# Row maxima one step later, turn and projections exchanged, seven PSUM banks for the last scores

## The chip, the cores and the metric

The kernel runs on one core of a Trainium2 chip. The metric is the device time of one execution in microseconds (us), the median of several. The core's engines work from queues of their own and wait for each other by semaphores: TensorE (PE; its weight loads are PEld), VectorE (DVE), ScalarE (ACT), GpSimd (POOL) and SyncE (SP), which issues most DMAs.

## The reference, cut to what matters

Sixteen sequences of 512 tokens, 128 features, 16 heads of 8 elements. Attention whose weights are the mean of the softmax and the softmax with key 0 taken out; output projection; residual; layer norm. Then a layer of eight experts, two for each token, and a second residual and layer norm.

```python
Q, K, V = heads(x @ Wq.T + bq), heads(x @ Wk.T + bk), heads(x @ Wv.T + bv)
probs = softmax(Q @ K.T / sqrt(8))
cut = probs with key 0 set to 0, divided by its sum
x1 = layernorm(x + ((probs + 0.5 * (cut - probs)) @ V) @ Wo.T + bo)
for e in 8 experts:   # wte: weights of the two chosen experts
    out += wte[:, e] * ((silu(x1 @ w1[e].T) * (x1 @ w3[e].T)) @ w2[e].T)
result = layernorm(x1 + out)
```

## The kernel before, in words

**Units and periods.** A unit is four heads of one sequence (`UNITS` is 64; unit u is group g = u % 4 of sequence b = u // 4). The loop runs over periods p from -2 to 63, each of eight steps k; two steps, an even and the odd one after it, are called a pair below. In period p the engines take the exponentials of unit p (16 score blocks of 128 keys by 512 queries, two to a step), the products with the values of unit p - 1 (four 128-key chunks, one in each odd step), and the row maxima of unit p + 2 (four parts of 128 queries, one in each even step).

**Row maxima.** A part is four matmuls of 32 contracted rows into the four banks of `mx_ps` (L635) and one VectorE reduction over all four banks (L1019). There is one such set of banks: the matmuls of a part wait for the reduction of the part before, and the reduction waits for the matmuls. When a unit's four parts are reduced, PE turns them to rows (`negmax_to_rows`, L666, "the turn"), ACT copies them (L846), POOL splits them in two bf16 parts (`split_negmax`, L1383 and L1385), and SP moves them by two 4 KB DMAs (`move_negmax`, L485) to two rows of the query operand. The first score matmul of the unit waits for that move (`s_m_loaded`).

**Order within a step.** It is written out: on PE the maxima of an even step, one score, the values of an odd step, the second score, the turn, and then one small piece named in `BEHIND` by (g, k), or in `ONCE` for the first periods: `q0` to `k1` are halves of a later sequence's projections, `v0`, `v1` value halves, `wo0`, `wo1` output halves, `px` prefix sums, `gc`, `gw` products for the gate. Scores, turns and pieces share a ring of three PSUM banks in order (`ring_at`, `bank_of`); ACT empties each bank, and PE waits for the emptying three entries back.

**Before the loop proper.** In periods -2 and -1 there are maxima and no scores; PE runs eight spare matmuls behind each part (L727). The piece `q0` of sequence 2 in period -1 needs the load of that sequence's `xT`, which SP issues behind the loads of the score operands of units 0 and 1 (L421 behind L478 and L479).

**GpSimd.** Its work of a period lies in four slots. A slot begins when PE has finished that step's maxima (`beside_reduction(p, w)`), so that it runs while VectorE reduces from PSUM. In periods of group 0, slot 1 holds the split of the maxima and a scatter, slot 2 holds `split_rest` (L1405, L1407) of a later sequence. VectorE runs routing operations of an earlier sequence after the reductions (L1077, L1081, L1086 in group 0).

**SyncE.** In order in each period: the move, loads of x or xT or the storing of split projections, the score operands of unit p + 5, the maxima operands of unit p + 4.

**After the loop.** In periods 62 and 63 there are no maxima. VectorE works out the table of expert tiles (`first_tables`, `tile_steps`, `tile_rows`), SP then loads the first rows, VectorE turns them (L1295), ACT copies the first weights, and PE goes on with the expert tiles, whose first product (`tile_up`, L755) writes into `mx_ps`.

Of the kernel before, what the change touches and what calls it, by code (L numbers as in the profile page):

```python
# [25 lines left out]
P = 128  # L26
# [32 lines left out]
def layer(nc, xT, x, wqT, wkT, wvT, woT, bq, bk, bv, bo, gateT, w1T, w3T, w2T, out):  # L59
# [16 lines left out]
    with ctx:  # L76
# [199 lines left out]
        UNITS, STEPS = NB * NG, 2 * QC  # L276
        PERIODS = range(-2, NB * NG)
# [4 lines left out]
        def is_seq(b):  # L282
            return 0 <= b < NB

        BEHIND = {(0, 3): ("k1", 2), (1, 3): ("v0", 1), (1, 5): ("v1", 1), (1, 7): ("px", -2),
                  (2, 5): ("wo0", -1), (2, 7): ("wo1", -1), (3, 3): ("q0", 3), (3, 5): ("q1", 3), (3, 7): ("k0", 3)}
# [11 lines left out]
        for p in PERIODS:  # L300
            for k in range(STEPS):
# [4 lines left out]
                if k == 1 and is_unit(p + 1):  # L306
                    ring_at["mT", p + 1] = ring_count
                    ring_count += 1
# [17 lines left out]

        def half(name):
            return slice(L // 2 * int(name[1]), L // 2 * (int(name[1]) + 1))

        def bank_of(n):  # L330
            return ring_ps[n % 3 if n < TAIL else 2][:, 0, :]
# [284 lines left out]
        def _(pe):  # L616

            def ring_bank(*what):

                n = ring_at[what]  # L620
                if n >= 3:
                    pe.wait_ge(s_ring_done, n - 2 if n < TAIL else n)
# [95 lines left out]
            for p in PERIODS:  # L718
                b, g = divmod(p, NG)
                for k in range(STEPS):  # L720
                    c = k // 2
                    if k % 2 == 0 and is_unit(p + 2):
                        maxima(p + 2, c)
                        if p + 2 in (0, 1):

                            for n in range(8):
                                nc.tensor.matmul(acc_ps[:, 0, :], QM[p + 2][:, 0:P], KM[p + 2][:, :], start=True, stop=True)  # L727
# [11 lines left out]
                    if k == 1 and is_unit(p + 1):  # L739
# [83 lines left out]
        def _(act):  # L823
# [100 lines left out]
            for p in PERIODS:  # L924
                b, g = divmod(p, NG)
                for k in range(STEPS):
# [3 lines left out]
                    if k == 1 and is_unit(p + 1):  # L930
# [54 lines left out]
        def _(dve):  # L985
# [226 lines left out]
            for p in PERIODS:  # L1212
                b, g = divmod(p, NG)
                for k in range(STEPS):
                    if k == 0 and is_unit(p - 2):
                        sums_by_query(p - 2)
                    if k % 2 == 0 and is_unit(p + 2):
                        maxima(p + 2, k // 2)
# [126 lines left out]
        def _(pool):  # L1345
# [235 lines left out]
            beside_reduction(-1, 1)  # L1581
# [4 lines left out]
            for p in PERIODS[2:]:  # L1586
# [3 lines left out]
                if g == 0:  # L1590
# [3 lines left out]
                    beside_reduction(p, 1)  # L1594
                    if is_unit(p + 1):
                        split_negmax(p + 1)
                    scatter_chunk(b - 3, 0)
                    beside_reduction(p, 2)
# [6 lines left out]
                elif g == 1:  # L1605
# [5 lines left out]
                    if is_unit(p + 1):  # L1611
                        split_negmax(p + 1)
# [3 lines left out]
                    beside_reduction(p, 2)  # L1616
                    if is_seq(b - 1):
# [7 lines left out]
                elif g == 2:  # L1625
# [5 lines left out]
                    if is_unit(p + 1):  # L1631
                        split_negmax(p + 1)
# [112 lines left out]
```

## Time and profile before

| | |
|---|---|
| median of 3 runs | 1175.48 us (1175.12 to 1177.51) |
| profiled execution | 1174.36 us, of which the span from the first to the last instruction is 1171.9 |
| PE busy | 1117.2 us (95%) |
| DVE busy | 911.3 us (78%) |
| ACT busy | 824.7 us (70%) |
| POOL busy | 689.8 us (59%) |

The shares are means over stages that differ. The second part of the page shows them over time, each digit the busy share of a fortieth of the span in tenths; PEclk is TensorE's granted clock:

```profile
PE   9999999999999999999999999999999999999996
DVE  6888999999999999999999999854545554444545
ACT  2588888888889889888889888853544344344537
PEclk9999999999999999999999999999999999999998
```

The main loop ends in slice 27 (about 764 us); until there PE and DVE are both nearly full, after it PE alone.

### The profile page before, as it was taken

The numbers are of one execution on the slowest core, as the hardware profiler recorded it, in microseconds if no ns is written. First come the engines' busy times: TensorE is split into PE (matmuls) and PEld (weight loads), VectorE is DVE, ScalarE is ACT, GpSimd is POOL, SyncE is SP. The second block draws the span as 40 slices with busy tenths as digits, with TensorE's granted clock in tenths as the row PEclk, the third lists the DMA queues.
The fourth block names the chain that finished last, engine by engine and source line by source line (L and its number), as shares of the span: only waits on it lengthen the run. The fifth ranks groups of instructions, "written<-read, shape, count | busy, mean of one in ns | idle before, by whom it ended". The sixth has DMA issues, their size and how long they took to land.

```text
span 1171.9 us, 23608 instructions
## 1 busy us (share of the span) xinstructions
PE 1117.2 (95%) x7240; PEld 575.9 (49%) x7240; DVE 911.3 (78%) x1309; ACT 824.7 (70%) x1668; POOL 689.8 (59%) x1131
## 2 busy tenths in 40 slices
PE   9999999999999999999999999999999999999996
PEld 6422232222222222222322222279999999999962
DVE  6888999999999999999999999854545554444545
ACT  2588888888889889888889888853544344344537
POOL 4424557777777776777777755676645434334336
PEclk9999999999999999999999999999999999999998
DMA  4453334444334343443444345353434433332257
GB/s 147 147 158 111 109 119 125 129 124 132 126 122 132 123 131 108 144 123 116 136 121 133 123 136 166 93 117 80 94 78 99 90 78 76 76 75 59 59 158 299
DMA packets 175051, 139.79 MB, mean 119 GB/s; under 512 B 89539, under 2 KB 151623, under 8 KB 174928
## 3 DMA queue, kind: packets, MB, share of 16 engines
q1 hardware_dynamic: 165672, 119.95, 36.4%
q0 software_dynamic: 8688, 18.14, 4.6%
q8 instruction: 60, 0.98, 0.4%
q14 instruction: 63, 0.52, 0.1%
q10 hardware_dynamic: 568, 0.20, 0.1%
HBM read 95.96 MB, written 42.19 MB: 118 GB/s over the span
## 4 chain that ended last, share of the span: by engine, by line
PE 54%; DVE 37%; issue 6%; DMA 1%; ACT 1%; ACTq 0%; POOL 0%; SPq 0%; POOLq 0%; DVEq 0%
DVE rowmax_sb L1019 32%; PE ring_ps L786 10%; PE mx_ps L755 10%; PE mx_ps L765 10%; PE ring_ps L646 6%; PE acc_ps L658 6%; PE mx_ps L635 4%; DVE TN_sb L1028 3%; PE mx_ps L817 2%; PE ring_ps L693 1%; PE ring_ps L676 1%; PE acc_ps L717 1%; PE ring_ps L817 1%; PE acc_ps L727 1%; DVE attnT_sb L1046 0%
## 5 line engine op out<-in xcount | busy, mean ns | idle before, releaser
L840 ACT ACTIVATE probs_sb<-ring_ps 128x512 f32<-128x512 f32 x1024 | 558.4, 598 | 96.0 <-PE ring_ps L646 80.7
L1019 DVE TENSOR_REDUCE rowmax_sb<-mx_ps 128x4 f32<-128x2048 f32 x256 | 586.5, 2291 | 40.9 <-PE mx_ps L635 32.6
L646 PE MATMUL ring_ps<-region_sb 74*128 74x512 bf16 x1024 | 311.4, 384 | 2.1 <-ACT probs_sb L840 2.0
L658 PE MATMUL acc_ps<-probs_sb,values_sb 128*32 128x512 f32 x2048 | 272.3, 604 | 0.0
L1694 POOL DMA_INDIRECT y_d<-probs_sb,values_sb x135 | 133.1, 986 | 183.8 <-DVE probs_sb L1313 159.3
L646 PEld LDWEIGHTS ring_ps<-region_sb 74*128 74x128 bf16 x1024 | 79.3, 97 | 312.8 <-ACT probs_sb L840 272.4
L915 ACT ACTIVATE xT_sb<-region_sb 128x512 f32 x78 | 49.2, 630 | 183.2 <-PE mx_ps L765 181.8
L1313 DVE SCALAR_TENSOR_TENSOR probs_sb<-ring_ps,values_sb 128x128 f32<-128x128 f32 x135 | 42.2, 347 | 147.3 <-issue 126.3
L1547 POOL DMA_INDIRECT rows_d<-sent_sb,pos_sb x128 | 130.3, 1018 | 40.2 <-issue 19.2
L635 PE MATMUL mx_ps<-k_maxima_sb,q_maxima_sb 32*128 32x512 bf16 x1024 | 101.0, 385 | 39.4 <-DVE rowmax_sb L1019 39.0
L786 PE MATMUL ring_ps<-region_sb,probs_sb 128*128 x1080 | 134.1, 276 | 0.3 <-DVE probs_sb L1323 0.3
L786 PEld LDWEIGHTS ring_ps<-region_sb,probs_sb 128*128 128x128 f32 x1080 | 131.0, 192 | 3.7 <-issue 0.5
L755 PE MATMUL mx_ps<-k_parts_sb,xT_sb 128*128 128x256 f32 (+1 forms) x624 | 130.2, 351 | 0.0
L1323 DVE TENSOR_TENSOR probs_sb<-mx_ps,probs_sb 128x512 f32<-128x512 f32 (+1 forms) x156 | 95.4, 619 | 25.4 <-PE mx_ps L765 17.7
L755 PEld LDWEIGHTS mx_ps<-k_parts_sb,xT_sb 128*128 128x128 f32 x624 | 106.8, 191 | 12.4 <-DVE k_parts_sb L1295 0.8
L658 PEld LDWEIGHTS acc_ps<-probs_sb,values_sb 128*32 128x32 f32 x2048 | 40.5, 108 | 97.7 <-issue 97.4
L635 PEld LDWEIGHTS mx_ps<-k_maxima_sb,q_maxima_sb 32*128 32x128 bf16 x1024 | 25.7, 91 | 110.7 <-DVE rowmax_sb L1019 101.8
L961 ACT ACTIVATE probs_sb<-mx_ps 128x1024 f32<-128x1024 f32 (+1 forms) x78 | 70.4, 903 | 3.5 <-PE mx_ps L755 3.4
L765 PE MATMUL mx_ps<-k_parts_sb,full_q_sb 128*128 128x256 f32 (+1 forms) x312 | 65.5, 353 | 0.0
L765 PE MATMUL mx_ps<-k_parts_sb,full_k_sb 128*128 128x256 f32 (+1 forms) x312 | 64.6, 350 | 0.0
L1383 POOL CAST negmax_parts_sb<-negmax_sb 16x128 bf16<-16x128 f32 x64 | 17.9, 280 | 64.4 <-PE mx_ps L635 64.2
L765 PEld LDWEIGHTS mx_ps<-k_parts_sb,full_q_sb 128*128 128x128 f32 x312 | 51.6, 191 | 5.3 <-issue 0.8
(197 smaller groups left out, 1182.2 us busy)
## 6 DMA issues: line engine op xcount, KB each, us to landing
region_sb<-q_parts_d SPq DMA_DIRECT2D x64, 288.0 KB
region_sb<-k_parts_d SPq DMA_DIRECT2D x64, 288.0 KB
k_parts_d<-k_parts_sb SPq DMA_DIRECT2D x46, 256.0 KB, 2.5
k_maxima_sb<-k_parts_d SPq DMA_DIRECT2D x128, 64.0 KB
probs_sb<-y_d SPq DMA_DIRECT2D x32, 256.0 KB, 6.8
q_maxima_sb<-q_parts_d SPq DMA_DIRECT2D x126, 64.0 KB
values_sb<-rows_d SPq DMA_DIRECT2D x57, 132.0 KB
q_parts_d<-q_parts_sb SPq DMA_DIRECT2D x15, 384.0 KB, 3.6
```

The source lines that it names most:

```text
L635: last = nc.tensor.matmul(mx_ps[:, j, :], q[rows, P * c:P * (c + 1)], k[rows, :], start=True, stop=True)
L646: nc.tensor.matmul(bank, KS[b % 2][0:KR + MR, h, P * c:P * (c + 1)], QS[b % 2][0:KR + MR, h, :], start=True, stop=True).then_inc(s_ring_re ...
L658: last = nc.tensor.matmul(acc_ps[VW * j:VW * (j + 1), 0, :], VE[b % 2][:, c, HG * g + j, :], PT[u % 2][:, j, c, :], start=(c == 0), stop=( ...
L755: last = nc.tensor.matmul(up_ps[:, c, 0:n], W1T[t % 2][:, P * c:P * (c + 1)], XGT[t % 2][:, 0:n], start=True, stop=True)
L765: last = nc.tensor.matmul(lin_ps[:, c, 0:n], W3T[t % 2][:, P * c:P * (c + 1)], XGT[t % 2][:, 0:n], start=True, stop=True)
L786: last = nc.tensor.matmul(y_ps[:, at:at + D], HH[t % 2][:, c, P * w:P * (w + 1)], W2[:, bass.ds(expert + c * D, D)], start=(c == 0), stop= ...
L840: nc.scalar.activation(PT[u % 2][:, i // QC, i % QC, :], ring_bank("st", u, i), ACT.Exp, scale=SCALE).then_inc(s_ring_done, 1)
L961: nc.scalar.activation(SG[t % 2][:, :, 0:n], up_ps[:, :, 0:n], ACT.Silu).then_inc(s_silu, 1)
L1019: V.tensor_reduce(rowmax[u % 2][:, :].rearrange("p (j c) -> p j c", c=QC)[:, :, c], mx_ps[:, :, :], axis=AXX, op=ALU.max, negate=True).the ...
L1323: V.tensor_tensor(HH[t % 2][:, part, 0:n], lin_ps[:, part, 0:n], SG[t % 2][:, part, 0:n], ALU.mult)\
L1547: G.indirect_dma_start(rows_d, bass.IndirectOffsetOnAxis(ap=pos[b % 2][:, s, c:c + 1], axis=0), XE[b % 2][:, c, s, :], None).then_inc(s_sc ...
L1694: G.indirect_dma_start(y_d, bass.IndirectOffsetOnAxis(ap=XG[t % RING][:, w, D:D + 1].bitcast(i32), axis=0), YO[t % YRING][:, w, :], None, ...
```

## The change: what it does, and the diff

Each maxima part comes one even step later: part c of period p is now part 7 + c of the unit count (`maxima_at`), so period p holds the last part of unit p + 1 and the first three of unit p + 2. The first one falls on step 2 of period -2, behind `gc`; the last one on step 0 of period 62. The turn goes from step 1 to step 3, and the pieces `k1`, `v0`, `q0` go from step 3 to step 1 of their periods. POOL's split of the maxima goes from slot 1 to slot 2. The scores of units 62 and 63 but the last six go over seven banks, the three of the ring and the four of `mx_ps`; the first four that use `mx_ps` wait for all reductions, and the first expert product waits for the last of these scores to be emptied.

```diff
+        LEAD = 2 * QC - 1
+        def maxima_at(p, c):
+            n = QC * p + c + LEAD
+            return divmod(n, QC) if 0 <= n < QC * UNITS else (None, None)
-        BEHIND = {(0, 3): ("k1", 2), (1, 3): ("v0", 1), (1, 5): ("v1", 1), (1, 7): ("px", -2),
-                  (2, 5): ("wo0", -1), (2, 7): ("wo1", -1), (3, 3): ("q0", 3), (3, 5): ("q1", 3), (3, 7): ("k0", 3)}
+        BEHIND = {(0, 1): ("k1", 2), (1, 1): ("v0", 1), (1, 5): ("v1", 1), (1, 7): ("px", -2),
+                  (2, 5): ("wo0", -1), (2, 7): ("wo1", -1), (3, 1): ("q0", 3), (3, 5): ("q1", 3), (3, 7): ("k0", 3)}
-                if k == 1 and is_unit(p + 1):        # ring_at, PE and ACT: the turn
+                if k == 3 and is_unit(p + 1):
+        WIDE = range(ring_at["st", UNITS - 2, 0], TAIL - 6)
+        banks_at = [WIDE[0] % 3, (WIDE[0] + 1) % 3, (WIDE[0] + 2) % 3, 3, 4, 5, 6]
+        def bank_no(n):
+            return banks_at[(n - WIDE[0]) % 7] if n in WIDE else n % 3
+        def last_in_bank(n):
+            return max(m for m in range(n) if bank_no(m) == bank_no(n))
         def bank_of(n):
-            return ring_ps[n % 3 if n < TAIL else 2][:, 0, :]
+            bank = bank_no(n) if n < TAIL else 2
+            return ring_ps[bank][:, 0, :] if bank < 3 else mx_ps[:, bank - 3, :]
             def ring_bank(*what):                    # PE
-                if n >= 3:
-                    pe.wait_ge(s_ring_done, n - 2 if n < TAIL else n)
+                if n in WIDE[3:7]:
+                    pe.wait_ge(s_mx_done, QC * UNITS)
+                elif n >= 3:
+                    pe.wait_ge(s_ring_done, last_in_bank(n) + 1 if n < TAIL else n)
-                    if k % 2 == 0 and is_unit(p + 2):  # PE; DVE alike
-                        maxima(p + 2, c)
-                        if p + 2 in (0, 1):
+                    u, part = maxima_at(p, c)
+                    if k % 2 == 0 and u is not None:
+                        maxima(u, part)
+                        if p < 0:
                             for n in range(8):
...
             def tile_up(t):
                 if t >= 1:
                     pe.wait_ge(s_silu, t)
+                else:
+                    pe.wait_ge(s_ring_done, WIDE[-1] + 1)
             def beside_reduction(p, w):              # POOL
-                if is_unit(p + 2):
-                    pool.wait_ge(s_mx_ready, QC * (p + 2) + w + 1)
+                u, part = maxima_at(p, w)
+                if u is not None:
+                    pool.wait_ge(s_mx_ready, QC * u + part + 1)
-            beside_reduction(-1, 1)                  # ahead of split_negmax(0)
+            beside_reduction(-1, 2)
                     beside_reduction(p, 1)           # group 0; groups 1 to 3 alike
-                    if is_unit(p + 1):
-                        split_negmax(p + 1)
                     scatter_chunk(b - 3, 0)
                     beside_reduction(p, 2)
+                    if is_unit(p + 1):
+                        split_negmax(p + 1)
                     if is_seq(b + 2):
                         split_rest(b + 2, 0)
```

## Rows read from the trace of the kernel before

**Rows 1.** Windows: busy us (instructions) by engine, then PEclk, DMA share, GB/s
```profile
200.00:400.00 200.00, 190.51 (x1270) 56.76 (x1268) 191.44 (x193) 174.78 (x372) 146.65 (x258) 1.00 0.40 125
...
800.00:900.00 100.00, 100.00 (x613) 92.17 (x612) 50.57 (x135) 45.48 (x67) 56.24 (x75) 1.00 0.39 86
```
**Rows 2.** Timeline, PE, a group 3 period: start us, us, what [idle before]
```profile
304.35 0.39 PE L635 MATMUL mx_ps<-k_maxima_sb,q_maxima_sb 32*128 32x512 bf16 x4 [0.29 <-DVE rowmax_sb L1019]
...
307.18 0.40 PE L635 MATMUL mx_ps<-k_maxima_sb,q_maxima_sb 32*128 32x512 bf16 x4
```
**Rows 3.** Timeline, PE, the start up to period 1
```profile
17.22 0.39 PE L635 MATMUL mx_ps<-k_maxima_sb,q_maxima_sb 32*128 32x512 bf16 x4
...
19.29 0.28 PE L682 MATMUL ring_ps<-gate_sb,centre_sb 128*128 128x8 f32 x2
...
20.02 0.40 PE L635 MATMUL mx_ps<-k_maxima_sb,q_maxima_sb 32*128 32x512 bf16 x4 [0.17 <-DVE rowmax_sb L1019]
...
29.17 0.39 PE L635 MATMUL mx_ps<-k_maxima_sb,q_maxima_sb 32*128 32x512 bf16 x4
...
34.03 0.59 PE L676 MATMUL ring_ps<-xT_sb,wq_sb 128*128 128x256 f32 x2
...
40.36 0.40 PE L635 MATMUL mx_ps<-k_maxima_sb,q_maxima_sb 32*128 32x512 bf16 x4
...
51.95 0.82 PE L646 MATMUL ring_ps<-region_sb 74*128 74x512 bf16 x3
```
**Rows 4.** Timeline, SP's queue, the start: xT of sequence 2, move of unit 1
```profile
25.81 0.34 SPq L421 DMA_DIRECT2D xT_sb<-xT  x1
...
45.35 1.22 SPq L485 DMA_DIRECT2D region_sb<-negmax_parts_sb  x2
```
**Rows 5.** Windows, the start: columns as in rows 1
```profile
26.00:28.00 2.00, 2.00 (x13) 0.81 (x13) 1.41 (x1) 0.72 (x2) 1.54 (x2) 1.00 0.88 223
```
**Rows 6.** Line 485, the move: landing from 45 to 46.5, then from 300 to 420
```profile
DMA to landing us min/median/max: 2.3/3.6/4.9
...
DMA to landing us min/median/max: 1.7/1.7/2.6
```
**Rows 7.** Timeline, POOL, a group 0 period: the split, then split_rest
```profile
316.22 0.28 POOL L1383 CAST negmax_parts_sb<-negmax_sb 16x128 bf16<-16x128 f32 x1 [1.03 <-PE mx_ps L635]
316.57 0.42 POOL L1385 TENSOR_TENSOR negmax_parts_sb<-negmax_sb,negmax_parts_sb 16x128 bf16<-16x128 f32 x1
...
319.72 1.15 POOL L1407 TENSOR_TENSOR q_parts_sb<-full_q_sb,q_parts_sb 128x512 bf16<-128x512 f32 x1
```
**Rows 8.** Timeline, DVE, the same period
```profile
318.99 2.29 DVE L1019 TENSOR_REDUCE rowmax_sb<-mx_ps 128x4 f32<-128x2048 f32 x1
...
321.41 0.19 DVE L1081 SCALAR_TENSOR_TENSOR dist_sb<-logits_sb,top_sb 128x32 f32<-128x32 f32 x1
...
321.79 2.29 DVE L1019 TENSOR_REDUCE rowmax_sb<-mx_ps 128x4 f32<-128x2048 f32 x1
```
**Rows 9.** Timeline, POOL and DVE side by side in period 63
```profile
755.31 1.27 POOL L1475 TENSOR_TENSOR ysum_sb<-attn_out_sb,x_sb 128x512 f32<-128x512 f32 x1
...
755.76 0.88 DVE L1169 TENSOR_TENSOR k_maxima_sb<-tile_no_sb,k_maxima_sb 1x45 f32<-1x45 f32 x1
```
**Rows 10.** Timeline, PE, ACT and DVE, the end of the loop
```profile
741.31 0.39 PE L635 MATMUL mx_ps<-k_maxima_sb,q_maxima_sb 32*128 32x512 bf16 x4 [0.33 <-DVE rowmax_sb L1019]
...
743.98 1.09 PE L646 MATMUL ring_ps<-region_sb 74*128 74x512 bf16 x3
...
764.45 1.89 PE L755 MATMUL mx_ps<-k_parts_sb,xT_sb 128*128 128x256 f32 x8
...
756.81 2.07 ACT L840 ACTIVATE probs_sb<-ring_ps 128x512 f32<-128x512 f32 x4 [0.33 <-PE ring_ps L646]
...
762.53 0.63 ACT L915 ACTIVATE xT_sb<-region_sb 128x512 f32 x1 [0.33 <-issue]
...
762.47 0.45 DVE L1295 STREAM_TRANSPOSE k_parts_sb<-q_maxima_sb 128x256 f32<-128x256 f32 x1 [2.67 <-DMA q_maxima_sb<-rows_d]
```

More of the change, by code:

```diff
@@ L721, in _ @@
                     c = k // 2
-                    if k % 2 == 0 and is_unit(p + 2):
-                        maxima(p + 2, c)
-                        if p + 2 in (0, 1):
+                    u, part = maxima_at(p, c)
+                    if k % 2 == 0 and u is not None:
+                        maxima(u, part)
+                        if p < 0:
                             for n in range(8):
-                                nc.tensor.matmul(acc_ps[:, 0, :], QM[p + 2][:, 0:P], KM[p + 2][:, :], start=True, stop=True)
+                                nc.tensor.matmul(acc_ps[:, 0, :], QM[u][:, 0:P], KM[u][:, :], start=True, stop=True)
                     if is_unit(p):
@@ L738, in _ @@
                         scores(p, 2 * k + 1)
-                    if k == 1 and is_unit(p + 1):
+                    if k == 3 and is_unit(p + 1):
                         negmax_to_rows(p + 1)
@@ L929, in _ @@
                         exp_chunk(p, 2 * k + 1)
-                    if k == 1 and is_unit(p + 1):
+                    if k == 3 and is_unit(p + 1):
                         negmax_rows(p + 1)
@@ L1216, in _ @@
                         sums_by_query(p - 2)
-                    if k % 2 == 0 and is_unit(p + 2):
-                        maxima(p + 2, k // 2)
+                    u, part = maxima_at(p, k // 2)
+                    if k % 2 == 0 and u is not None:
+                        maxima(u, part)
                     if is_seq(b - 1):
@@ L1594, in _ @@
                     beside_reduction(p, 1)
+                    scatter_chunk(b - 3, 0)
+                    beside_reduction(p, 2)
                     if is_unit(p + 1):
                         split_negmax(p + 1)
-                    scatter_chunk(b - 3, 0)
-                    beside_reduction(p, 2)
                     if is_seq(b + 2):
@@ L1630, in _ @@
                     beside_reduction(p, 1)
-                    if is_unit(p + 1):
-                        split_negmax(p + 1)
                     if is_seq(b - 2):
@@ L1635, in _ @@
                     beside_reduction(p, 2)
+                    if is_unit(p + 1):
+                        split_negmax(p + 1)
                     if is_seq(b + 2):
@@ L1647, in _ @@
                     beside_reduction(p, 1)
-                    if is_unit(p + 1):
-                        split_negmax(p + 1)
                     if is_seq(b + 1):
@@ L1652, in _ @@
                     beside_reduction(p, 2)
+                    if is_unit(p + 1):
+                        split_negmax(p + 1)
                     if is_seq(b + 1):
```

## The prediction, written before the run

> **What bounds the kernel now.** Read the windows by stage first [rows 1]: in 200 us of the main loop PE is busy 190.5 and DVE 191.4, ACT 174.8; past the loop PE alone is full, 100.0 of 100, and DVE is half idle. So a change in the loop counts only where it moves both PE and DVE, and what it saves ahead of the first expert product comes off the end in full, since PE has no idle time afterwards in which it could be lost.
>
> Next the timelines of PE and DVE in the loop. A pair of steps has two floors. VectorE's: a reduction of 2.29, then the next part's matmuls, which need the banks, then the next reduction: 2.80 from one to the next [rows 8], more when DVE has over half a microsecond of other work between them. TensorE's: maxima, four scores, eight value matmuls and at most one piece; with a projection half 2.83, no idle, from 304.35 to 307.18 [rows 2]. Where the piece is only the turn PE waits, there 0.29 for the reduction [rows 2]. Four pairs make a period of about 11.3. Both floors are within 1% of each other; the loop has nothing to give but ends and accidents.
>
> **The start.** PE begins the maxima at 17.22, behind its warm-up, and the loop proper (first maxima of period 0) at 40.36 [rows 3]: eight parts, about 2.89 each. The change leaves seven. `gc`, today behind the first part, comes ahead of it: from 19.29 it takes to 20.02 less the 0.17 of waiting [rows 3], 0.55; the first part starts at 17.8. The next three pairs hold the same pieces as the three between 20.02 and 29.17 [rows 3], 9.15: part four at 26.9. Its pair has two projection halves, 3.05 like the mean of those three, and three more at 2.80 follow: period 0 would begin at 38.4 for 40.36, a gain of 2.0.
>
> Two loads stand against it. First, `q0` of sequence 2 moves up a pair with the exchange and a pair with the lead. PE comes to it 2.07 (maxima and spare matmuls, 17.22 to 19.29 in rows 3) and a projection half of 0.4 after 26.9, at 29.4. Its xT is issued at 25.81 today [rows 4] and first used at 34.03 without a wait [rows 3]. SyncE can issue it some 1.5 earlier, since the piece it waits for comes earlier, but not before the four operand loads of units 0 and 1, which stand ahead of it. Those are 1.18 MB by their shapes and xT is 0.26; at 223 GB/s [rows 5] 1.44 MB takes 6.5, and these loads share the engines with what follows. Bounds: 27.2 (no wait) and 34.0 (a wait of 4.6). I take 30.5, since the queue is 0.88 full on all engines then [rows 5] and moving the issue earlier doesn't move a queue that never runs dry: a wait of 1.1.
>
> Second, the move of unit 1. Today its two DMAs are issued from 45.35 on [rows 4], right behind the loads of SyncE's round, and the slowest lands 4.9 after its issue [rows 6]; if that is the second, issued 0.6 after the first, it lands at 50.9, one microsecond before the first score of period 1 at 51.95 [rows 3]. In the new order POOL's split of unit 0 waits for the second part of unit 1, which by the sum above (with the wait for xT) is 1.3 later than today, and the stores, the operand loads and this move queue behind that on POOL and SP: landing 52.2. The score would come at 51.95 - 0.9 = 51.05: a wait of 1.15. Bounds: none, and 2. Behind a waiting score PE holds all of its queue, the next maxima among it, so both waits go into the loop whole. Start: -2.0 + 1.1 + 1.15 = +0.2; bounds -2.0 and +0.9 (the larger xT wait would take part of the second one with it).
>
> **The loop.** The turn still has three steps between its last reduction and itself. `q0` and `v0` trade pairs with it at no cost: the pair they leave falls from 2.83 to 2.80 and the pair they enter rises by as much. `k1` leaves a pair in which DVE's three routing operations already take 2.83 by themselves: +0.03 in 14 sequences, +0.4 (0 to 0.5).
>
> The split and its move have less time. In a period of group 0 the split ends at 316.99 [rows 7] and its second DMA lands about 2.3 later (0.6 of issue, 1.7 to land, rows 4 and 6), at 319.3; the next period's first score is two pairs behind the reduction of 318.99 [rows 8], near 324.5. The room falls from 5.1 to 2.3, still more than nothing, so I cost it at zero; it is the loop's new weak point. The loads that follow the move in SyncE's queue come as much later; xT is issued 2.8 later and used 2.8 earlier, and still has 5 us to land.
>
> Now POOL's slots. In slot 2 of group 0 the split goes ahead of `split_rest`. It takes 0.74 (0.36 from cast to subtraction and 0.42 of that, less a little overlap [rows 7]), so the subtraction of L1407, today 319.72 to 320.87, becomes 320.46 to 321.61. VectorE's L1081, which reads two SBUF tensors, starts at 321.41 [rows 8]. Such operations do not run side by side: a DVE operation on 45 elements that started at 755.76, under a POOL operation of 1.27 from 755.31, took 0.88 and ended at 756.64, 0.06 after POOL's [rows 9]. So L1081 ends between 321.67 and 321.80 instead of 321.60, and with it the chain to the next reduction at 321.79 [rows 8], on which PE waits too: 0.07 to 0.20 a period, in the 12 sequences that have both operations. I take 0.13: +1.6, bounds 0 (DVE gets in first) and 12 x 0.29 = 3.5 (all that POOL overruns the reduction with).
>
> The Trainium skill (SBUF — State Buffer, Who interferes with whom) says that a VectorE instruction with two SBUF inputs contends with a GpSimd instruction that reads SBUF, and that whichever issues first holds the shared ports for the whole instruction. The row of 0.88 agrees. By the rule alone L1081 would start at 321.61, 0.20 a period, 2.4 in all.
>
> In slot 2 of group 1 the split shifts POOL's normalisation by the same 0.74 towards DVE's two routing operations there, but that pair waits for PE's `v1` anyway by 0.3: 0, up to 0.1 x 14. In groups 2 and 3 what DVE runs after slot 2 reads one tensor. Loop: +2.0 (0 to 5).
>
> **The end.** Today PE goes from 743.98 (first score of period 62) to 764.45 (first expert product): 20.5 for eight pairs, 2.4 each and some pieces [rows 10]. ACT's four exponentials take 2.07 and then ACT waits 0.33 for PE [rows 10]: the ring of three empties while PE is at its values. With seven banks that wait goes, and ACT's rate of 0.49 (a third of 2.07 less 0.6) counts. But the last maxima part now stands at the head: 741.31 [rows 10] + 2.87 = 744.2. The fourth score waits for its reduction, 0.45 + 2.29 + 0.1 after the maxima, so its exponential starts at T + 3.3 (T for 744.2); 26 of them to the one that frees the last score's bank (the last six scores have three banks again) at 0.49 are 12.7, the turn, two output drains and two weight copies of 0.6 [rows 10] 1.8, and PE's own values delay it by some 0.4: last score at T + 18.2, expert product at T + 18.4: 762.6. The product also needs the first rows turned, today at 762.47 + 0.45 [rows 10], behind the table chain on DVE. That chain would start behind the 256th reduction instead of behind POOL, by the sums above up to half a microsecond sooner, so this gate opens between 762.4 and 762.9. I take 762.75 for 764.45: -1.7. Bounds: -2.3, and 0 where the table comes 1.5 later.
>
> **Sum.** +0.2 + 2.0 - 1.7 = +0.5 us: the profiled execution's 1174.36 would be 1174.9. The median of the runs shown lies 1.1 above that execution; on it the same sum gives 1176.0.
>
> **Rivals.**
> A. The start keeps its pair: xT lands by 29.4 and the move by 51. For it: the shares in rows 5 are means, an early issue might find engines free. Against: a landing of 4.9 in rows 6. Then -2.0 + 2.0 - 1.7 = -1.7, and where the ports cost nothing as well -3.3: 1172.2 to 1173.8. Chance 0.15.
> B. DVE gets in ahead of POOL, or POOL's op ends early enough: the loop costs 0.4. Then -1.1: 1174.4. Chance 0.20.
> C. Slower: VectorE is shut out in group 0 and in group 1. Place: the routing operations after slot 2. It decides where POOL's operation is still under way when DVE's begins. Price 0.29 x 12 + 0.2 x 14 = 6.3 instead of 1.6, so +5: 1180.6. The same size follows if moves land after over 4 us (2.3 of room on top of 1.7), as in rows 6 at the start: 0.9 in each of 16 group 0 periods. For it: margins counted in tenths; against: operations there overran nothing so far. Chance 0.12.
> D. The end gives nothing back, since the table and the first rows gate the product: +0.5 + 1.7 = +2.2, 1177.7. For it: the two gates are within 0.5. Against: DVE is no busier than before once the 256th reduction is over. Chance 0.13.
>
> **How the numbers follow.** The forecast has 0.40. A difference under 0.2%, 2.35 us, is about what cannot be told from none here. Faster: most of A and a little of B, 0.14. Slower: C, and the upper third of D and of the forecast's loop bound, 0.18. Same: 0.68. The range takes in B and D, and half of A: 1173.2 to 1178.4.
>
> **What would show it.** First score of period 0 near 39.8, with PE waiting about a microsecond ahead of `q0` near 30; first score of period 1 waiting for its move until about 52. In group 0 periods the time from the third to the fourth reduction 2.93 for 2.80, and L1081 longer than 0.19; all other pairs within 0.04 of today's. From the 256th maxima to the first expert product 18.4, and no idle 0.33 on ACT there. It is wrong if period 0 begins before 39, if no DVE operation grows, if scores wait at the head of ordinary periods, or if the granted clock leaves 1.00 during the new waits at the start.

## The result and the profile after

The changed kernel takes 1179.33 us (median of 22 runs, 1175.95 to 1181.99) where the kernel before took 1175.83 on the same chip: ratio 1.0027, 95% interval 1.0021 to 1.0033. It is 3.5 us slower, outside the forecast's range. The profiled execution took 1179.18, its span is 1177.3 for 1171.9. One run of the kernel before, at 1791.74, counts neither in the ratio nor in the spreads. Eighteen further runs follow; each ratio is to the kernel before, run beside it on the same chip.

The stages first, as in [rows 1]: the windows of the changed kernel, busy us by engine (PE, PEld, DVE, ACT, POOL), PEclk, DMA share, GB/s.

```profile
200.00:400.00 200.00, 190.38 (x1270) 57.36 (x1272) 191.04 (x192) 173.87 (x372) 146.59 (x254) 1.00 0.41 128
780.00:880.00 100.00, 100.00 (x614) 92.16 (x613) 50.04 (x123) 47.12 (x73) 59.33 (x86) 1.00 0.40 86
```

Loop and expert stage look as before. The loss is at the start, and the timeline of PE shows it (start us, us, line, operands, in brackets the idle time ahead and what ended it); these rows answer to [rows 3].

```profile
27.18 0.39 PE L654 MATMUL mx_ps<-k_maxima_sb,q_maxima_sb 32*128 32x512 bf16 x4
27.51 1.90 PE L747 MATMUL acc_ps<-k_maxima_sb,q_maxima_sb 128*128 128x512 bf16 x8
29.25 0.59 PE L695 MATMUL ring_ps<-xT_sb,wk_sb 128*128 128x256 f32 x2
32.50 0.67 PE L695 MATMUL ring_ps<-xT_sb,wq_sb 128*128 128x256 f32 x2 [2.66 <-DMA xT_sb<-xT]
33.10 0.39 PE L654 MATMUL mx_ps<-k_maxima_sb,q_maxima_sb 32*128 32x512 bf16 x4
33.43 3.57 PE L747 MATMUL acc_ps<-k_maxima_sb,q_maxima_sb 128*128 128x512 bf16 x8
...
42.65 0.39 PE L654 MATMUL mx_ps<-k_maxima_sb,q_maxima_sb 32*128 32x512 bf16 x4
...
54.94 0.81 PE L665 MATMUL ring_ps<-region_sb 74*128 74x512 bf16 x3 [0.63 <-DMA region_sb<-negmax_parts_sb]
```

Up to 29.25 all comes as worked out (part four at 27.18 for 26.9, with 0.25 of later start). Then `q0` of sequence 2 waits 2.66 for its xT, and the same eight spare matmuls that took 1.90 take 3.57. The windows of those microseconds say why: the granted clock (the column behind POOL's) stayed at 1.00 in the wait and fell to 0.50, 1.2 of 2.4 GHz, after it.

```profile
30.00:32.00 2.00, 0.00 (x0) 0.00 (x0) 0.00 (x0) 0.35 (x1) 1.15 (x1) 1.00 0.79 183
...
33.00:34.00 1.00, 1.00 (x7) 0.37 (x7) 0.45 (x1) 0.47 (x1) 0.00 (x0) 0.75 0.76 209
34.00:35.00 1.00, 1.00 (x4) 0.30 (x2) 1.00 (x1) 0.00 (x0) 0.00 (x0) 0.50 0.74 201
35.00:36.00 1.00, 1.00 (x4) 0.36 (x3) 0.84 (x1) 0.00 (x0) 0.00 (x0) 0.50 0.71 197
...
37.00:38.00 1.00, 1.00 (x8) 0.41 (x8) 0.49 (x1) 0.27 (x1) 0.36 (x2) 1.00 0.06 16
```

SP's queue in the same stretch, beside [rows 4]: xT goes out 0.9 earlier than before, but behind the four operand loads of units 0 and 1; by the DMA view it lands 7.4 after its issue.

```profile
24.13 0.76 SPq L496 DMA_DIRECT2D region_sb<-k_parts_d  x1
24.93 0.51 SPq L438 DMA_DIRECT2D xT_sb<-xT  x1
```

To add this up I take the starts of VectorE's reductions (and, at the end, PE's last score and first expert product) from each timeline. "Start" is the 13 pairs from the seventh last reduction ahead of period 0 to the third of period 1; "loop" the 58 periods from there; the last two columns count from the reduction at which that loop ends (720.06 in the changed kernel).

```
                                start     loop   last score  first product
before                          37.34   658.64      47.78       48.01
changed                         42.30   659.28      46.87       48.04
changed, again                  44.48   659.26      47.20       47.43
xT first                        39.91   659.29      46.95       48.00
12 spare matmuls                41.14   663.73      47.19       47.50
three banks                     41.98   659.28      47.95       48.18
banks alone                     37.32   658.51      46.45       46.91
end order                       42.10   659.27      50.51       50.73
exchange alone                  40.33   659.04      47.80       48.03
exchange, order mended          37.49   658.29      47.81       48.04
changed, order mended           37.55   660.41      46.89       47.74
exchange, banks, order mended   37.48   658.27      45.93       46.82
```

Changed against before: the first reduction comes 0.81 later (18.48 for 17.67), one pair of 2.79 is not there, the start takes 4.96 more, the loop 0.64, the way to the product 0.03 more: 3.65, and 768.10 for 764.45 it is. Past the product the two executions differ by another 1.75; that stretch takes between 407.4 and 410.1 in the six profiles of kernels with lead eight that no transfer holds up, so I read nothing into it. The 4.96 are 2.66 of wait, 1.67 of slow spare matmuls and 0.63 of wait for the move of unit 1.

The loop beside [rows 7, 8], in the changed kernel: POOL's subtraction for `split_rest`, DVE's routing operation, the reductions around it.

```profile
323.95 1.16 POOL L1430 TENSOR_TENSOR q_parts_sb<-full_q_sb,q_parts_sb 128x512 bf16<-128x512 f32 x1
```

```profile
322.47 2.29 DVE L1041 TENSOR_REDUCE rowmax_sb<-mx_ps 128x4 f32<-128x2048 f32 x1
...
324.89 0.26 DVE L1103 SCALAR_TENSOR_TENSOR dist_sb<-logits_sb,top_sb 128x32 f32<-128x32 f32 x1
...
325.30 2.29 DVE L1041 TENSOR_REDUCE rowmax_sb<-mx_ps 128x4 f32<-128x2048 f32 x1
```

DVE's operation took 0.26 for 0.19 and ended 0.04 behind POOL's: it is held up by POOL's operation, at the small end of the forecast. The pair is 2.83 for 2.80; over the sequences of the loop its median is 2.82.

The end beside [rows 10]: first PE, then DVE.

```profile
747.73 0.39 PE L654 MATMUL mx_ps<-k_maxima_sb,q_maxima_sb 32*128 32x512 bf16 x4
...
750.70 0.61 PE L665 MATMUL mx_ps<-region_sb 74*128 74x512 bf16 x2 [0.83 <-DVE rowmax_sb L1041]
...
766.93 0.39 PE L665 MATMUL ring_ps<-region_sb 74*128 74x512 bf16 x1 [0.58 <-ACT probs_sb L862]
768.10 1.97 PE L777 MATMUL mx_ps<-k_parts_sb,xT_sb 128*128 128x256 f32 x8 [0.79 <-DVE k_parts_sb L1318]
```

```profile
767.55 0.45 DVE L1318 STREAM_TRANSPOSE k_parts_sb<-q_maxima_sb 128x256 f32<-128x256 f32 x1 [4.13 <-DMA q_maxima_sb<-rows_d]
```

The last score is 19.2 behind the last maxima, not 18.2, and then the product waits 0.79 for the first rows, whose loads SP issues at 764.25.

### The profile page after: what moved, and what is told of

It is laid out like the page before. It is cut to its first block, busy times and chain, and to the rows that moved or that the text cites. A ratio compares the mean times of both kernels' runs of the same rounds, so it can differ in the third digit from the quotient of the medians.

```text
span 1177.3 us, 23565 instructions
## 1 busy us (share of the span) xinstructions
PE 1117.3 (95%) x7232; PEld 575.8 (49%) x7232; DVE 907.7 (77%) x1309; ACT 824.0 (70%) x1668; POOL 689.8 (59%) x1131
## 4 chain that ended last, share of the span: by engine, by line
PE 58%; DVE 29%; issue 5%; DMA 3%; SPq 2%; POOL 1%; ACT 0%; DVEq 0%; POOLq 0%; ACTq 0%
DVE rowmax_sb L1041 26%; PE ring_ps L808 10%; PE mx_ps L787 9%; PE mx_ps L777 9%; PE ring_ps L665 9%; PE acc_ps L677 9%; PE mx_ps L654 6%; PE ring_ps L695 1%; DVE TN_sb L1050 1%; PE mx_ps L839 1%; PE ring_ps L712 1%; PE ring_ps L720 1%; PE ring_ps L839 1%; DMA xT_sb<-xT 1%; SPq L578 1%
## 5 line engine op out<-in xcount | busy, mean ns | idle before, releaser
L1041 DVE TENSOR_REDUCE rowmax_sb<-mx_ps 128x4 f32<-128x2048 f32 x256 | 585.0, 2285 | 46.5 <-PE mx_ps L654 41.5
L862 ACT ACTIVATE probs_sb<-ring_ps 128x512 f32<-128x512 f32 x1010 | 550.4, 598 | 96.2 <-PE ring_ps L665 78.5
L665 PE MATMUL ring_ps<-region_sb 74*128 74x512 bf16 x1010 | 306.5, 384 | 1.4 <-ACT probs_sb L862 0.8
```

Of the source, the lines that this page charges most:

```text
L665: nc.tensor.matmul(bank, KS[b % 2][0:KR + MR, h, P * c:P * (c + 1)], QS[b % 2][0:KR + MR, h, :], start=True, stop=True).then_inc(s_ring_re ...
L862: nc.scalar.activation(PT[u % 2][:, i // QC, i % QC, :], ring_bank("st", u, i), ACT.Exp, scale=SCALE).then_inc(s_ring_done, 1)
L1041: V.tensor_reduce(rowmax[u % 2][:, :].rearrange("p (j c) -> p j c", c=QC)[:, :, c], mx_ps[:, :, :], axis=AXX, op=ALU.max, negate=True).the ...
```

## The experiments

**Is it the start?** In the first variant xT goes out behind unit 0's operands alone:

```diff
-            for u in (0, 1):
-                load_qk(u)
+            load_qk(0)
             load_xT(2)
-            for u in (2, 3):
+            for u in (1, 2, 3):
                 load_qk(u)
```

> The changed kernel with one load moved on SyncE: xT of sequence 2 is issued behind the operand loads of unit 0, no longer behind those of units 0 and 1. Theory S (the loss is made at the start: `q0` of sequence 2 waits 2.66 us for xT, and TensorE's clock falls to 0.50 behind that wait): xT has 0.59 MB less ahead of it, lands some 2.6 us earlier, the wait is under 0.5, the clock stays at 1.00, the 8 spare matmuls behind `q0` take 1.90 again for 3.57, period 0 begins near 38.5 for 42.65, and the run is 3 to 4.3 us shorter than the changed kernel: 1175.0 to 1176.3. Rival L (the loss is in the loop, by VectorE shut out beside GpSimd): the start gets shorter but the time is given back, at most 0.5 us gained: 1178.8 to 1179.3. Rival B (the seven banks cost it): as rival L.

1175.56 us, ratio 0.9998 (0.9989 to 1.0006): 3.8 less than the changed kernel, within what theory S expected. xT lands 5.9 behind its issue and `q0` no longer waits:

```profile
29.78 0.59 PE L694 MATMUL ring_ps<-xT_sb,wk_sb 128*128 128x256 f32 x2
30.43 0.67 PE L694 MATMUL ring_ps<-xT_sb,wq_sb 128*128 128x256 f32 x2
```

Period 0 began at 39.43, not at 38.5, and its first score waited 0.85 for its own move; period 1's waited 1.20.

**The wait and the clock apart.** Here PE gets 12 more spare matmuls ahead of that `q0`:

```diff
+                        if (name, p) == ("q0", -1):
+                            for n in range(12):
+                                nc.tensor.matmul(acc_ps[:, 0, :], QM[u or 0][:, 0:P], KM[u or 0][:, :], start=True, stop=True)
                         if is_seq(b + off):
                             behind(name, b + off)
```

> The changed kernel with 12 more spare matmuls (128x512, 0.22 us each) on PE ahead of `q0` of sequence 2, so that PE works where it waited 2.66 us for xT; `q0` itself begins when it did. Theory S: the wait alone is 2.66, the fall of the clock behind it is another 1.7 (8 spare matmuls at 3.57 for 1.90); with the clock kept the first maxima of period 0 come 1.7 us earlier, near 41.0, and the run is 1.7 shorter: 1177.6. Rival W (the clock falls whatever PE does in those 3 us, or its fall is hidden by VectorE): no change, 1179.3, period 0 near 42.6. Rival L: the gain is lost in the loop, 1178.8 to 1179.3.

The start did as theory S said: `q0` at 32.00, clock at 1.00, the eight spare matmuls 1.90 again, period 0 at 40.91.

```profile
32.00 0.59 PE L695 MATMUL ring_ps<-xT_sb,wq_sb 128*128 128x256 f32 x2
...
32.85 1.90 PE L747 MATMUL acc_ps<-k_maxima_sb,q_maxima_sb 128*128 128x512 bf16 x8
```

But the whole took 1181.0 (ratio 1.0042, 1.0029 to 1.0054), 1.7 more than the changed kernel. No rival had that. The loop had grown by 4.4, all in pairs at the head of group 1 periods where a score waited for its move, the longest:

```profile
465.38 0.81 PE L665 MATMUL ring_ps<-region_sb 74*128 74x512 bf16 x3 [1.66 <-DMA region_sb<-negmax_parts_sb]
```

with the clock at 0.60 and 0.55 in the two windows behind it. What made the move late is in SP's rows. SP stores K's parts of a later sequence at 449.04, and the operand loads behind wait for the stores to land; they went out at 454.51, 5.5 later, for 3.8 in most sequences. Their 0.58 MB then stand ahead of the move of 459.03. The DMA view of one microsecond in those stores, in the run with 12 spare matmuls (queue, packets, MB, share of 16 engines):

```profile
q1 hardware_dynamic: 347, 0.34, 100.9%
q8 instruction: 1, 0.02, 5.9%
```

One 16 KB packet of an instruction queue holds one DMA engine for 5.9% of 16, 0.94 us, in the middle of the stores. In the changed kernel's own sequence (stores at 449.77, loads at 453.57) the packet comes when the stores are over, alone in the window 453.7 to 454.7:

```profile
DMA packets 1, 0.02 MB, mean 16 GB/s; under 512 B 0, under 2 KB 0, under 8 KB 0
...
q8 instruction: 1, 0.02, 7.4%
```

In four profiles (both runs with more work ahead of `q0`, the exchange alone and the changed kernel) all eight gaps of 4.9 or more had such a packet 0.9 to 2.7 us behind the stores' issue, and every packet of the queue 4.5 or more behind it left the gap at 3.8. In the nine other profiles with this order in SP's loop no gap came to 4.9; three of 4.12 to 4.39 had a packet 3.9 to 4.0 behind the stores' issue. So the packet goes with the long gap each time, but it was not produced at will. Nor is it shown that the extra instructions moved it: with them it came 2.0 to 2.7 earlier in three sequences and 5.8 in a fourth, but between the two profiles of the changed kernel one packet moved by 2.1 as well (4.57 and 6.68 behind the stores). Next a run that was to keep the number of PE's instructions:

> The changed kernel, PE kept at work in the wait for xT as in the run with 12 spare matmuls, but by 6 of f32 (128x512, 0.43 us each by the projection halves of 256 columns at 0.215), and 6 spare matmuls fewer in period 0, so that the number of PE's instructions stays that of the changed kernel. In the run with 12 the start was 1.5 us shorter and yet the whole slower: in 4 of its sequences the stores of K's parts took 5.0 to 5.6 until the load behind them went out, for 3.8, and the scores waited for late moves; in those stretches a 16 KB packet of the instruction queue lay inside the stores (2 us behind their issue, 4.5 to 6.6 in the changed kernel). Theory C (the extra instructions shifted PE's code loading onto the stores): here the gap is 3.8 in all sequences, no score waits inside the loop, and the run is 1.5 to 1.7 shorter than the changed kernel: 1177.7. Rival W (an earlier start by itself, or the kept clock, makes the moves late): waits as in the run with 12, 1180 to 1181.

This run, with 6 matmuls of f32 in place of the 12 and 6 spare matmuls fewer in period 0, took 1184.55 (1.0065, 1.0048 to 1.0083). It tells little: a 128x512 f32 matmul costs 0.86, recorded as two, not 0.43; `q0` came at 34.88, and gaps of 5.3 and 5.5 were there in two sequences, again with the packet inside. Neither theory's numbers came.

**The end.** Without the seven banks (`bank_no` returns `n % 3`, the two waits that go with them dropped), and the seven banks alone in the kernel before:

> The changed kernel without the seven banks: the scores of units 62 and 63 take turns over three banks as all others do. Theory E (the first expert product waits for the first rows, whose loads wait for the last scatters of sequence 12; so the banks give nothing): within 0.7 us of the changed kernel, first rows loaded at the same time behind the 256th maxima, exponentials with 0.33 of idle again. The prediction's term: 1.7 slower, 1181.0. Rival B (seven banks cost, since scores and maxima share them and the first of them wait for the last reduction): 1 to 2 faster, 1177.3 to 1178.3.

> The kernel before with the seven banks alone: the lead of eight parts and the order of turn and projections stay. The last maxima part is then over before unit 62 begins, so no bank is waited for. Prediction's rule: the ring no longer empties, and the product is gated by the first rows turned: 762.9 for 764.45, 1.5 faster, 1174.3. Theory E: the same gate decides, but the scatters and the table come where they did, so the gain lies between 0.5 and 1.5: 1174.3 to 1175.3. Rival B: slower than before by up to 1, 1176 to 1177.

Three banks in the changed kernel: 1178.87, ratio 1.0025 (1.0017 to 1.0034), the same as with seven, as theory E said. Seven banks in the kernel before: 1174.19, ratio 0.9987 (0.9978 to 0.9996), 1.5 faster, as the prediction's rule said (1174.95 and an interval up to 1.0001 when run again, below). By the table the banks bring the last score forward by 1.33 there and the product by 1.10; in the changed kernel the last score by 1.08 and the product by 0.14, the rest going into the wait for the first rows. So theory E said that the rows are worth hurrying: the last two scatters ahead of POOL's split of unit 63 and `add_bo`, DVE's table ahead of its drain of unit 61.

```diff
                         count_rows(b - 2)
                     beside_reduction(p, 2)
+                    if b == NB - 1:
+                        scatter_chunk(b - 3, 6)
+                        scatter_chunk(b - 3, 7)
                     if is_unit(p + 1):
                         split_negmax(p + 1)
...
```

> The changed kernel with two orders changed at the end: GpSimd issues the last two scatters of sequence 12 ahead of the split of unit 63 and of `add_bo` (755.20 and 757.71 become some 753.5 and 754.6), and VectorE lays the first table before it drains the output of unit 61, for which it waited 2.08. Theory E (the first expert product is gated by the first rows, which wait for scatters and table): first row loads near 761 for 764.25, rows turned near 764.5 for 767.55; then the last score decides, 766.93 as before, so the product comes at 767.4 for 768.10 and the next wait of 0.48 may stay: 0.7 to 1.2 shorter, 1178.1 to 1178.6. Rival D (the drain of unit 61 and the move of unit 63, both later, hold PE): last score later by 0.5 to 1, 1179.3 to 1180.3.

> The changed kernel with both: xT of sequence 2 behind the operand loads of unit 0 alone, and the two orders at the end. If the start and the end are separate terms: 1175.6 (xT first alone) less 0.7 to 1.2, 1174.4 to 1174.9, 0.5 to 1 below the kernel before. Rival: one of them moves what the other gains, 1175.3 to 1176.

1182.3 (1.0059, 1.0037 to 1.0081), and with xT first 1178.03 (1.0027, 1.0017 to 1.0038): each 2.5 to 3 slower than without. The first rows were loaded at 761.40 as hoped, but the move of unit 63 was now late:

```profile
759.94 0.62 PE L665 MATMUL mx_ps<-region_sb 74*128 74x512 bf16 x2 [2.16 <-DMA region_sb<-negmax_parts_sb]
...
770.33 0.39 PE L665 MATMUL ring_ps<-region_sb 74*128 74x512 bf16 x1 [0.58 <-ACT probs_sb L862]
```

with the clock at 0.54 from 761 to 764. Rival D, at over three times its size (the last score 3.6 later, where it had 0.5 to 1), and the same pair of costs as at the start: a wait and a slow clock behind it. Table and scatters were moved together, so which of the two had held the rows back stays open.

**The exchange alone.** Lead of eight parts as in the kernel before, three banks, turn and projections exchanged:

> The kernel before with the exchange alone: turn, split and move one pair later and `k1`, `v0`, `q0` one pair earlier, lead of eight parts, three banks. The prediction's loop term: +2.0, 1177.7, with the third pair of group 0 at 2.93 for 2.80. By the trace of the changed kernel: +0.03 a sequence and 0.4 once, +0.6 to +0.9, 1176.4; the start is that of before, since `q0` of sequence 2 comes near 31.2 and xT lands before. Rival M (moves one pair later land late now and then): some scores wait at the head of group 1 periods, 1178 and a wide spread.

1181.61, ratio 1.0048 (1.0031 to 1.0065): dearer than the whole change, where the trace of the changed kernel had promised 0.6 to 0.9. Its loop is 0.4 longer than before (659.04), its start 3.0. Ahead of period 1 PE waits for the maxima operands of unit 3, which SP issues from 46.34 on, behind the operand loads of unit 4 that had waited for the stores:

```profile
53.98 0.40 PE L652 MATMUL mx_ps<-k_maxima_sb,q_maxima_sb 32*128 32x512 bf16 x4 [1.77 <-DMA k_maxima_sb<-k_parts_d]
```

```profile
52.00:54.00 2.00, 0.23 (x5) 0.05 (x4) 0.70 (x1) 0.95 (x2) 0.28 (x1) 1.00 0.63 199
54.00:56.00 2.00, 2.00 (x11) 0.51 (x15) 1.51 (x1) 1.23 (x3) 0.00 (x0) 0.71 0.39 132
56.00:58.00 2.00, 2.00 (x11) 0.77 (x4) 0.79 (x1) 0.55 (x2) 0.00 (x0) 0.50 0.29 93
```

**All moves and operands in their order.** So the theory became: whatever PE needs soon must not stand behind score operands that are needed periods later (M). First try, in the changed kernel: moves ahead of operand loads, and these a round later.

> The changed kernel with another order on SyncE: xT of sequence 2 behind the operand loads of unit 0 alone, as in the run that moved it, and every move of the row maxima ahead of the score-operand loads that stood before it in SyncE's queue (the loads of units 2 and 3 behind the move of unit 0; from then on the loads of unit p+4 behind the move of period p, where those of unit p+5 stood at the end of it). Theory M (what the later turn costs is moves and operands that queue behind 0.58 MB loads, which themselves wait for the stores: 0.63 to 2.3 us at the heads of periods 0 and 1, and now and then in the loop where a packet of PE's code lies in the stores): from the first reduction to the seventh of the loop 37.5 us for 42.3 in the changed kernel and 39.9 with xT alone (37.3 in the kernel before), no score waits for a move anywhere, and the time is 2 below xT alone, 1173.5 (1172.5 to 1174.5), under the kernel before. Rival S (only xT matters): as with xT alone, 1175.6, or no better than the 1178.0 of xT with the end reordered.

1219.89, ratio 1.0376 (1.0340 to 1.0412). The operand load now stood ahead of xT in every group 2 round, which I had overlooked. From 45 us to 740 PE waited:

```profile
PE ring_ps L695 <- DMA xT_sb<-xT: 19.8, 13, 2.2
```

13 waits, 19.8 us, 2.2 the longest, and a loop 34.6 longer than that of the changed kernel, 2.7 for a wait of 1.5 in the mean. The mean hides two kinds. Behind six of the 13 waits (1.41 to 2.19) the clock fell, and their sequences are 2.8 to 6.4 longer than in the changed kernel; behind the first, at 77.10, the windows have it at 0.74 from 78 and 0.50 from 80. Behind the other seven (1.05 to 1.68) it stayed at 1.00, and their sequences are 1.3 to 1.9 longer, the wait and little else. So it fell after fewer than half, not after most, as the expectation of the next version has it. One of the seven, and the window behind it:

```profile
509.83 0.67 PE L695 MATMUL ring_ps<-xT_sb,wq_sb 128*128 128x256 f32 x2 [1.68 <-DMA xT_sb<-xT]
```

```profile
511.00:513.00 2.00, 2.00 (x13) 0.36 (x11) 2.00 (x1) 1.65 (x5) 1.18 (x1) 1.00 0.12 38
```

The exchange alone with this order, expected at 1175.0 to 1176.3, took 1218.93 (1.0354, 1.0334 to 1.0375), and PE waited for xT in it in the same way. Beside them the changed kernel again, on that chip, and the banks with this order:

> The changed kernel as it is, on the chip of these runs, so that the others are compared on one chip. Both theories: 1179.3 (1178 to 1181), 0.2 to 0.4% over the kernel before; q0 of sequence 2 waits 2 to 3 us for xT and the granted clock falls to 0.50 to 0.75 behind it.

> The kernel before with the seven banks and the same order on SyncE. Its turns are a pair earlier and no score waits for a move, so theory M expects nothing from the order beyond the banks alone: 1174.2 (1173.7 to 1174.7). If the order of loads costs something by itself (operands or stores later than they are needed), it is slower than that, 1175 or more, and then the run with the moves first pays the same.

The changed kernel: 1180.10 (1.0027, 1.0017 to 1.0038), as before; in this profile the wait for the move of unit 1 was 1.42, the clock fell to 0.50 from 56 to 58, and the start was 2.2 longer than in the first profile. The banks: 1174.64 (0.9985, 0.9976 to 0.9994), no price for the order where the turn is early and xT has time.

Then with xT ahead of the operands, in each round of SP (at the start, not shown, xT of sequence 2 behind unit 0's operands and those of units 2 and 3 behind the first moves):

```diff
                     move_negmax(p + 1)
+                if g == 2 and 2 < b + 3 < NB:
+                    load_xT(b + 3)
+                if p >= 0:
+                    for u in {0: (2, 3), 1: (4, 5)}.get(p, (p + 4,)):
+                        if is_unit(u):
+                            load_qk(u)
...
-                if is_unit(p + 5):
-                    load_qk(p + 5)
```

> The changed kernel with SyncE's order mended all through: in each round the move of the row maxima first, then xT where there is one, then the score operands (of units 2 and 3 in period 0, 4 and 5 in period 1, later of unit p+4, a round later than now), then the rest. In the first try xT stood behind the operands in each sequence: PE waited for it 13 times, 19.8 us in all, with TensorE's clock falling after most of them, 40 us lost. Theory M (each wait of PE for a transfer that queues behind operand loads costs itself and a fall of the clock; nothing else makes the change slower): no such wait is left, from the first reduction to the seventh of the loop 37.4 to 38.3 us for 42.3 in the changed kernel, the loop as in the changed kernel, 1173.0 to 1174.5, below the kernel before and xT alone. Rival L (the later turn costs by itself): the start is short, the time 1175.6 or more.

> The exchange alone (lead of eight parts, three banks; 1181.6 on its own) with SyncE's order mended in the loop: move, xT, score operands of unit p+4, the rest; the loads ahead of the loop as in the kernel before. Theory M: the maxima operands of unit 3, for which PE waited 1.77 ahead of period 1 with the clock at 0.50 for some 3 us behind it, go out ahead of the operands of unit 4 and land in time; no other wait for a transfer in the loop; 1174.5 to 1176.3, not slower than the kernel before. Rival L: 1178 or more.

The exchange alone went from 1181.61 to 1174.92 (0.9997, 0.9988 to 1.0006): rival L is out. No transfer holds PE up in its loop, and the move of unit 1 lands as fast as any later one (line 502, 46 to 50 us; [rows 6] has 2.3 to 4.9 there):

```profile
DMA to landing us min/median/max: 1.7/1.7/1.7
```

The change itself went to 1175.43 (0.9998, 0.9989 to 1.0007), level with the kernel before, 0.9 above the range of theory M (1173.0 to 1174.5): the start is the 37.55 forecast, period 1 is 2.2 ahead of the kernel before, but one score (period 3) waited 1.08, and the product again 0.85 behind the last score. Beside it, on one chip:

> xT of sequence 2 first, alone, as run before (1175.6, ratio 0.9998), on this chip. Theory M: 1175 to 1178, between the changed kernel and the one with the whole order mended, with a spread of its own, since the waits at the heads of periods 0 and 1 are left (0.85 and about 1) and it hangs on their length whether the clock falls. Rival S (xT is all): 1175.6 and as narrow as the kernel before.

> The kernel before with the seven banks alone, as run before (1174.2, ratio 0.9987), on this chip. Both theories: 1174 to 1174.8, 1.0 to 1.8 below the kernel before. If the kernel with the whole order mended is below this one, the shorter start is worth its price.

1176.62 (1.0003, 0.9994 to 1.0012), as theory M had it, and 1174.95 (0.9992, 0.9983 to 1.0001), 0.15 above its range. In xT first the score of period 1 now waited 0.84 and the clock did fall, to 0.50.

Last, two versions to win more: operands of one unit a round and the last scatter ahead of `add_bo`; and exchange, banks and order with the lead of eight.

> The changed kernel with SyncE's order mended (move, xT, score operands of one unit a round, of unit p+2, the rest) and the last scatter of sequence 12 issued ahead of GpSimd's `add_bo`. Theory M with the start's pair worth its price: start as in the last run (37.5 us from the first reduction to the seventh of the loop), no wait for a move in the loop, first rows loaded at least 1 us sooner behind the last reductions than in the changed kernel, so the first product waits for the last score alone: 1.1 + 0.7 below the last run's 1175.4, 1173.6 (1173.0 to 1174.5). Rival: the end does not follow, or a wait shows up elsewhere: 1175 or more.

> Exchange, seven banks and the mended order with the lead of eight parts left. Theory M: the exchange costs nothing with this order and gives 0.35 in the loop (658.29 against 658.64), the banks give what they gave alone (1.0 to 1.5): 1173.8 to 1174.7. Rival: with the later turn the last move is late at the end and the banks give nothing: 1175.5.

1175.26 (0.9994, 0.9985 to 1.0003): the wait in the loop is gone, but the start took 38.45 for the 37.5 expected (PE idle 0.65 until `q0` at 30.46, its xT landing at 30.33), `px` at 745.39 waited 1.49 for POOL, with the clock at 0.50 behind it, and the last score stands at 50.70 by the table's count for 46.89; the rival. And 1174.06 (0.9993, 0.9983 to 1.0003), inside its forecast. The four runs with banks and lead eight took 1174.06 to 1174.95, the exchange with the order mended and without the banks 1174.92. Only the first run of the banks alone and the banks with the moves first have intervals that end below one; the others can't be told from the kernel before.

## Why the prediction was wrong, by its own steps

**The pair saved at the start, -2.0: right.** A pair of 2.79 is gone, `gc` stands ahead of the first part for some 0.5, and with no wait left the 13 pairs of the start take 0.21 more (37.55 for 37.34): about 2.

**The wait for xT, 1.1: mis-sized, the step that failed.** I took 30.5 for the landing of a load behind 1.18 MB, from 223 GB/s, with 34.0 as the bound; it was issued 0.9 earlier than before, where I had 1.5, and landed at 32.4, so the wait was 2.66. And I priced a wait as a wait. "If the granted clock leaves 1.00 during the new waits at the start" stood among the signs of being wrong, with no price: the slow clock behind the wait cost another 1.67. Without it the time would have been some 1177.7, inside the range (an estimate, 1179.33 - 1.67).

**The wait for the move, 1.15: right mechanism, 0.63, but it varies.** The sum had a slip: by its own terms the second part of unit 1 comes at 33.85 for 31.97, 1.9 later and not 1.3, which makes the wait 1.75. It was 0.63, 1.42 in the second profile, 0.84 and 1.20 with xT first; 1.42 and 0.84 took the clock with them, 0.63 and 1.20 did not. That is where the runs' spread of 6 us, for 3.4 before, can come from: the mean granted clock of each of the 22 runs is 0.997 in the two shortest (1175.95 and 1176.10) and 0.994 in the longest (1181.99), though which wait it fell behind only a profile tells.

**The loop, +2.0: +0.64.** `k1` and its exchange cost nothing: with the order mended the exchange makes the loop 0.35 shorter. VectorE was held up beside GpSimd by 0.07 on the operation, 0.02 on the pair, where I took 0.13. In the exchange alone with the order mended the same operation took 0.33 and its pair 2.89, near what I took, and even so that loop is the shorter one. Costing the later moves at zero held in these profiles of the changed kernel, but the margin is what the run with 12 spare matmuls fell through; that is the second half of rival C, with a cause I did not see.

**The end, -1.7: 0.03.** The gate I named, first rows turned, did decide, but 20.3 behind the last maxima part where I had 18.2 to 18.7 (the bound of 0 stood for a table 1.5 late): scatters issued at 755.20 and 757.71, behind a split that now comes a pair later, and a table that waited 2.08 for unit 61's output. The last score too came 1.0 later than worked out (19.2 for 18.2). That is rival D. Loop and end erred by -1.4 and +1.7 and nearly cancelled; the start, +3.0 for +0.2, is the miss.

The Trainium skill (DMA: Bandwidth & Descriptors, Queues, rings and completion order) says that the descriptors of one ring are taken in order and that a transfer's semaphore lands only after the earlier writes of that DMA engine, from all its queues. The traces agree: a 4 KB move landed 1.7 after its issue where SP had issued nothing for 3.6 ahead of it, and one behind 0.58 MB of score operands and the maxima operands kept a score waiting until 5.1 after its issue (49.82 to 54.94).

## What to carry to other kernels

When a consumer moves earlier, look at what stands ahead of its transfer in the same queue, not only at when the transfer may be issued: order a queue by when the data is needed. Price a wait of the matmul engine twice, with the clock kept and with the slow clock behind it: here 2.66 cost 1.67 more, and among the 13 waits for xT those with a fall cost 2.8 to 6.4 a sequence, those without 1.3 to 1.9. A gate at the end with half a microsecond to spare is a second bound, not a detail.

## What the hardware showed that was not expected

The clock's fall does not follow from the length of the one wait ahead of it: it fell behind waits of 0.84, 1.42, 1.66, 1.77 and 2.66, and stayed at 1.00 behind others of 0.63, 1.20 and 1.68. What tells them apart these runs do not settle.

Queues that the profile calls instruction queues show up on the DMA engines, the larger one with 61 packets of 16 KB in most runs, each 0.9 to 1.7 us on one engine. In all eight cases where one came 0.9 to 2.7 behind the issue of the stores, the loads that wait for these stores went out 1.1 to 1.7 later than usual.
